# A two-layer graph network on one core: block order on TensorE, an earlier target term, and a cast that changes engine

## The reference

```
def _mp_layer(x, src, dst, edge_attr, W, b):
    # self loops with zero edge_attr are appended: src2, dst2, ea2
    msg = concat([x[dst2], x[src2], ea2], axis=1) @ W + b
    agg = segment_sum(msg, dst2, num_segments=n)
    return relu(agg)
h   = relu(_mp_layer(x, src, dst, edge_attr, W1, b1))     # 64 -> 128
out = _mp_layer(h, src, dst, edge_attr, W2, b2)           # 128 -> 64
y   = log_softmax(out, axis=1)
return layernorm(x + y, axis=-1)
```

## Time and profile before

| what | value |
|---|---|
| profiled execution, device time | 207.35 us |
| its span in the trace | 205.5 us |
| median of three runs | 207.33 us |
| PE busy, matmul | 174.7 us (85%) |
| DVE busy | 174.2 us (85%) |
| ACT busy | 118.8 us (58%) |
| POOL busy | 49.6 us (24%) |

### The profile page before, as it was taken

How to read it: one execution, slowest core, us unless ns; L and a number is a source line. 1 busy time by engine, 2 the same in 40 slices (tenths; PEclk the granted TensorE clock), 3 DMA queues, 4 the chain that set the end, 5 groups by cost and what they waited for, 6 DMA issues and landing times.

```text
span 205.5 us, 5089 instructions
## 1 busy us (share of the span) xinstructions
PE 174.7 (85%) x2019; PEld 162.7 (79%) x2019; DVE 174.2 (85%) x495; ACT 118.8 (58%) x234; POOL 49.6 (24%) x58
## 2 busy tenths in 40 slices
PE   0414489899999999999899999999996999999940
PEld 0103389778989999889789999898996999999940
DVE  1899999999999999999999989921029999999873
ACT  2236658679898998898798989984310201121101
POOL 8388998403200594006004000000000000000000
PEclk9999999999999999999999999999999999999995
DMA  1334101000000000000000000000000010011000
GB/s 42 102 85 131 25 0 40 0 4 2 3 0 4 0 5 0 3 1 3 0 4 0 5 0 3 2 3 0 3 0 0 3 35 6 6 38 25 22 22 20
DMA packets 8886, 3.32 MB, mean 16 GB/s; under 512 B 8146, under 2 KB 8411, under 8 KB 8861
## 3 DMA queue, kind: packets, MB, share of 16 engines
q1 hardware_dynamic: 8061, 2.04, 4.8%
q0 software_dynamic: 800, 0.93, 1.8%
HBM read 2.15 MB, written 0.81 MB: 14 GB/s over the span
## 4 chain that ended last, share of the span: by engine, by line
DVE 51%; PE 38%; issue 4%; ACT 2%; DMA 2%; ACTq 0%; DVEq 0%
PE pset L1022 17%; DVE ohr L517 17%; DVE ohl L517 16%; PE acc L1022 7%; PE acc L981 6%; PE pset L967 4%; DVE adj L507 3%; DVE u L548 2%; DMA adj<-in_dst 2%; DVE adj L466 1%; PE epb L1008 1%; PE epb L1016 1%; PE epb L996 1%; DVE x L533 1%; DVE u L556 1%
## 5 line engine op out<-in xcount | busy, mean ns | idle before, releaser
L820 ACT ACTIVATE adj<-pset 125x1000 bf16<-125x1000 f32 (+7 forms) x100 | 81.1, 836 | 14.1 <-PE pset L967 12.0
L981 PE MATMUL acc<-x,adj 125*125 125x195 bf16 x625 | 67.4, 250 | 0.0
L967 PE MATMUL pset<-ohr,ohl 128*125 128x125 bf16 x625 | 53.9, 230 | 9.2 <-DVE ohr L517 8.7
L967 PEld LDWEIGHTS pset<-ohr,ohl 128*125 128x125 bf16 x625 | 48.0, 145 | 14.9 <-issue 5.8
L981 PEld LDWEIGHTS acc<-x,adj 125*125 125x125 bf16 x625 | 56.7, 138 | 0.3
L517 DVE TENSOR_TENSOR ohl<-iota,keys 128x1000 bf16<-128x1000 bf16 (+1 forms) x79 | 52.4, 664 | 0.6 <-ACT keys L803 0.5
L517 DVE TENSOR_TENSOR ohr<-iota,keys 128x1000 bf16<-128x1000 bf16 (+1 forms) x79 | 52.5, 664 | 0.0
L1022 PE MATMUL pset<-z,adj 125*125 125x192 bf16 x425 | 36.9, 246 | 1.8 <-DVE x L665 1.8
L1022 PEld LDWEIGHTS pset<-z,adj 125*125 125x125 bf16 x425 | 35.6, 136 | 2.4 <-DVE x L665 2.0
L909 ACT ACTIVATE x<-x 125x192 f32<-125x192 f32 (+2 forms) x6 | 2.6, 428 | 34.5 <-DVE x L674 34.5
L387 POOL CAST stats<-se 125x15 bf16<-125x15 f32 x5 | 4.8, 952 | 52.8 <-DMA se<-se_scratch 52.8
(11 more groups left out here) (122 smaller groups left out, 171.4 us busy)
## 6 DMA issues: line engine op xcount, KB each, us to landing
x_nat<-in_x_tiles SPq DMA_DIRECT2D x1, 406.2 KB
x_nat<-in_x_tiles SPq DMA_DIRECT2D x1, 375.0 KB
out<-x SPq DMA_DIRECT2D x2, 187.5 KB
out<-x SPq DMA_DIRECT2D x3, 93.8 KB
adj<-in_dst SPq DMA_DIRECT2D x1, 208.5 KB
out<-x SPq DMA_DIRECT2D x1, 125.0 KB
adj<-in_edges,adj POOLq DMA_INDIRECT x5, 4.9
adj<-in_edge_attr,adj POOLq DMA_INDIRECT x5, 3.4
```

What stands on the lines that cost most here:

```text
L820: ins = act.activation(adj4[0:Q, g, :, i * WD:(i + n) * WD].rearrange("p h (w e) -> p h w e", e=WD), rows[:, w - k * SET:w - k * SET + n, ...
L967: ins = pe.matmul(pset[k % 2][0:Q, i // 4, i % 4 * 128:i % 4 * 128 + WD * G], ohl[k % 3][:, i // 2, :, i % 2], ohr[k % 3][:, i // 2, :, i ...
L981: ins = pe.matmul(acc[g % 2][0:Q, 0:XW], adj4[0:Q, g, h, :], x3[:, h, :], start=(h == 0), stop=(h == G - 1))
```

## The change

Five edits, in the order of the program:

- the cast of the targets is made by ScalarE (an activation with a bias) where it was a VectorE operation;
- on VectorE `onehots(4)` moves in front of `attr_sums(0)`, which moves behind `low_of_x(1)`;
- on TensorE `layer1` of block b stands in front of `build(b + 4)`, for every block, and the wait of group 0 on x is split in two;
- `base_of` is called for groups 0 to 11 and 12 to 15 right after the last `reduce_sums`, and for 16 to 24 after the first batch; the wait on `rest_ready` in front of it goes;
- the last step of a batch is one subtraction and one multiplication over all its groups, with the subtraction put between two small operations on the variance.

```diff
-            dve.tensor_scalar(rows16[:, 0:EC], dst_rows[:, 2:EC + 2], -float(MID), None, ALU.add).then_inc(rowsf_ready, 1)
...
-            attr_sums(0, 0, WD)
             onehots(3)
             low_of_x(1, XA, G)
-
-            for k in range(4, NSETS):
+            onehots(4)
+            attr_sums(0, 0, WD)
+
+            for k in range(5, NSETS):
...
             reduce_sums(G - 1)
+            dve.wait_ge(b2_in, 16 * 2)
+            for j in range(J):
+                dve.wait_ge(se_in[j], 16)
+            base_of(0, BATCHES[1][1])
+            base_of(BATCHES[1][1], BATCHES[2][1])
             z_rest(last - 1)
...
-            dve.wait_ge(rest_ready, len(EPILOGUES))
-            base_of(0, BATCHES[1][1])
...
-                flink(dve.tensor_tensor(r, y, y, ALU.mult))
+                fpost(dve.tensor_tensor(r, y, y, ALU.mult))
+                dve.wait_ge(fch, fc[0] - 1)
+                flink(dve.tensor_tensor(o, p, c.unsqueeze(2).broadcast_to([Q, n, C]), ALU.subtract))
...
-                for k in range(n):
-                    ins = dve.tensor_scalar(f_v[i % 2][:, k, :], f_p[:, k, 0:C], f_c[:, k:k + 1], f_r[:, k:k + 1],
-                                            ALU.subtract, ALU.mult)
-                flink(ins)
+                flink(dve.tensor_tensor(vv, o, r.unsqueeze(2).broadcast_to([Q, n, C]), ALU.mult))
...
-                    base_of(BATCHES[1][1], G)
+                    base_of(BATCHES[2][1], G)
...
+            act.wait_ge(dst_in, 16)
+            act.activation(rows16[:, 0:EC], dst_rows[:, 2:EC + 2], ACT.Copy, bias=-float(MID)).then_inc(rowsf_ready, 1)
...
                     if g == 0:
-                        pe.wait_ge(xl_ready, 2)
+                        pe.wait_ge(xm_ready, 1)
+                        pe.wait_ge(xl_ready, 1)
                         pe.wait_ge(keys_ready, 1)
...
+                    if g == 0 and h == XA:
+                        pe.wait_ge(xm_ready, 2)
+                        pe.wait_ge(xl_ready, 2)
...
             for b in range(NSETS):
-                if b + LEAD < NSETS:
-                    build(b + LEAD)
                 i, end = b * SET, b * SET + set_size(b)
                 while i < end:
...
+                if b + LEAD < NSETS:
+                    build(b + LEAD)
```

More of the change, by code:

```diff
@@ L619, in _ @@
             z_low(last - 2)
[L620 to L625, removed]
             fc = [0]
@@ L650, in base_of @@
                 flink(dve.tensor_tensor(base[:, a:b, :], base[:, a:b, :], late_part, ALU.add))
+            reduce_sums(G - 1)
             dve.wait_ge(b2_in, 16 * 2)
@@ L654, in _ @@
                 dve.wait_ge(se_in[j], 16)
-            dve.wait_ge(rest_ready, len(EPILOGUES))
             base_of(0, BATCHES[1][1])
+            base_of(BATCHES[1][1], BATCHES[2][1])
+            z_rest(last - 1)
+            z_low(last - 1)
+            z_rest(last)
+            z_low(last)
+            dve.tensor_reduce(deg_sum[:, :], stats[:, :, 0], AX.X, ALU.add).then_inc(deg_ready, 1)
             na = 0
```

## The result

| | kernel before | changed kernel |
|---|---|---|
| median device time | 207.29 us (207.03 to 207.69) | 223.21 us (222.76 to 223.76) |
| ratio to before, 95% interval | | 1.0768 (1.0753 to 1.0784) |
| profiled execution, its span | 207.35 us, 205.5 us | 223.76 us, 222.0 us |
| PE / DVE / ACT busy | 174.7 / 174.2 / 118.8 us | 177.8 / 175.9 / 119.0 us |

A forecast was written before the change was run, and what follows sets the result against it. VectorE (51%) and TensorE (38%) were taken to share the chain, TensorE with 7 us spare in the loop. Sum: 207.35 + 18.1 (waits) - 0.5 (start) - 1.07 (cast) - 1.81 (target) - 0.13 (last step) = 222.0 us; range 213 to 230.

The forecast's parts named there:

- What bounds the kernel: Layer-1 loop: VectorE and TensorE share the chain; TensorE has 7 us to spare, 5.0 of it for new waits.
- Group starts: Layer 1 of groups 1 to 24 waits for ScalarE's evacuation, no longer covered by other TensorE work: 19.2 us in sum.
- price 1.36 - 0.086 p: Wait in us of a group that begins p matmuls into its layer-1 block, until its evacuation is done.
- turn_sums: Epilogues in the loop: its wait of about 0.25 us for scale_x grows by 0.69 in six; +3.9 us.
- Head start: Start of the loop: layer 1's block 0 runs ahead of build 4, while TensorE waits for one-hots; -0.5 us.
- The order of attr_sums: Start, on VectorE: moving attr_sums(0) leaves the sum of work up to one-hot 5 as it was; nothing.
- The cast: Start: with dst cast on ScalarE, VectorE begins its picks at once and TensorE starts sooner; -1.07 us.
- Target term: Layer 2: base_of fits VectorE's hole of 5.91 us, and TensorE's wait ahead of group 6 goes; -1.81 us.
- Last step: End of the last batch: the stretch of 1.35 us becomes 1.22; -0.13 us.
- Hidden waits: Rival for the loop: VectorE bounds it, TensorE's new waits cost nothing, and the kernel takes 204.3 us; 7%.
- The clock: Rival for the loop: pauses at each group drop TensorE to 1.2 GHz for a third of 75 sets; +15, 237 us; 5%.
- backlog: Rival for the loop: ScalarE falls behind, 15 group starts each meeting one more cast; +7.5, 229.5 us; 12%.

The follow-up runs named there:

- build-first version: Changed kernel with one edit undone, build(b + 4) again in front of layer 1 of block b in all blocks: 204.63 us, ratio 0.9867.
- the kernel with block 0 alone: Changed kernel with layer 1 in front of the build in block 0 only and the build first in blocks 1 to 78: 204.78 us, ratio 0.9875.
- last experiment: Changed kernel with build(b + 4) again in front of layer 1 in all blocks and the cast of dst back on VectorE: 205.34 us, ratio 0.990.

## Why the prediction was right

By its own steps:

- *What bounds the kernel.* 7 us of spare time for TensorE was the number that decided, and the traces bear it out. From the first layer-1 matmul to the first of layer 2 the build-first version took 115.2 us and the changed kernel 135.1, that is 19.8 more. The new waits in this stretch are 25.0 us (20.4 + 5.3 - 0.7) less the 1.4 of group 0, which lie ahead of it: 23.6. The stretch also holds one build more, about 0.9 us, since layer 1 of block 0 now begins before it. So about 4.7 us were absorbed; 5.0 had been allowed. Between 27.1 and 141.3 us the kernel before has above all these waits of builds, and the changed kernel has none from its first layer-1 matmul on:

```profile
PE pset L967 <- DVE ohr L517: 2.3, 5, 0.8
PEld pset L967 <- ACT adj L820: 3.1, 7, 1.0
```

- *Group starts.* Forecast 19.2 us in 24 places, measured 20.4 in 22 by the idle time of the weight loads, of which one is group 0's own 1.4: 19.0 for the rest. (The rows of the matmuls give 16.2 in 20, since their modelled ends reach into the wait.) By the distances between starts the three parts of the forecast come out one by one: 16.2 us for the 16 groups that pay in full (16.3 forecast), 1.7 for the seven behind an epilogue (2.1), 0.7 for group 24 (0.8). The price 1.36 - 0.086 p holds where it was read: 1.25 us at p = 1 (1.27 by the list), and 78.30 + 0.17 to 79.64, 1.17, at p = 2 (1.19).

```profile
78.30 0.33 PE L986 MATMUL acc<-x,adj 125*125 125x195 bf16 x2
...
79.64 0.56 PE L986 MATMUL acc<-x,adj 125*125 125x195 bf16 x4 [1.01 <-ACT adj L821]
```

- *turn_sums.* Forecast +3.9 us in six epilogues, measured 0.7 to 5.3 in six, +4.6. The wait that it had before was read too large: 8 x 0.25 = 2.0, where the list has 0.7 in three.
- *Head start.* Forecast -0.5. Layer 1 does begin 0.8 us sooner than in the build-first version (24.79 against 25.61), but by the kernel with block 0 alone it is worth nothing in the end.
- *The order of attr_sums.* Forecast nothing, and nothing it is: 0.85 us won at the first layer-1 matmul, together with the split wait on x, and 1.14 lost behind it (last experiment). The prediction did not see that the loop would be the longer for it.
- *The cast.* Forecast -1.07, and the start gained 0.56. This term was mis-sized by half. The step that failed is that VectorE would be done with its picks by as much sooner as the cast had taken. The first pick took 0.64 us where the same shape takes 0.25 later. All 14 traces show why the length of the operation did not matter: what VectorE begins at that moment ends at a fixed time. The cast on VectorE began at 4.55 to 4.87 us in five traces, took 1.20 to 0.89, and ended at 5.75 to 5.77 in each. With the cast on ScalarE the first pick began at 4.66 to 5.04 in seven traces, took 0.92 to 0.54, and ended at 5.57 or 5.58 in each; in the other two it ended at 5.21, and the first row matmul came at 5.75 instead of 6.11, which is the 0.91 us of the cast alone. So it did not matter either that the targets landed 0.13 us later in this execution (4.73 against 4.60). GpSimd has a row of memsets from 4.25 to 5.5 us in all of them (to 5.6 in those two); that it is the cause was not tested.
- *Target term.* Forecast -1.81, measured -2.3 alone, and -2.13 for the whole last part with the last step's 0.13 in it.
- *Last step.* Forecast 1.22 us, measured 1.21. Alone it can't be told from nothing, as its size said. By the estimate from the rule of the Trainium skill ("VectorE: DVE Perf Modes", the perf-mode tier table) it would have lost 0.1 us; the trace has it 0.14 shorter than the 1.35 before.
- *The rivals.* Hidden waits (204.3 us) is what the kernel gives once the order is undone, 204.6, so its price was right and its condition was not met. The clock stayed at its upper level: the granted clock is 1.00 from 31 to 160 us, and a build takes 72.98 to 73.47, 0.49 us, right between pauses of a microsecond. With six sets ahead it did fall, so the rival's mechanism exists in this kernel, at pauses of 1.6 to 1.9 us. For the slow first blocks (0.86 us for a build) the prediction names the lower level; the profile gives 1.00 for 27.0 to 29.7 us, so that reading rests on the spacing alone. ScalarE had no backlog; over 64 to 84 us its busy time fell from 18.00 to 14.70.

The net: +18.63 at the first layer-2 matmul was forecast as +16.5 (-1.07 - 0.5 + 18.1). The loop grew by 21.0 us (114.1 to 135.1) and not by 18.1, and its start came 2.35 us sooner and not 1.57. The 2.9 us in the loop are about 0.5 of waits, 0.3 less absorbed, 0.9 for the build that moved into it, and 1.1 that the order of `attr_sums` gives back. So the result within 0.6% of the forecast owes something to luck: two errors of opposite sign, 2.9 and 0.8 us.

## What to carry to other kernels

In a software pipeline over serial engine lists, moving a consumer by one place against its producers changes the cover of every wait in the loop, not that of the first round alone: list what stands between each producer and its consumer, and price the difference against the spare time of the engine that waits. Where two engines are both near full, spare time is a few per cent and a wait of one evacuation in each group costs nearly all of itself. A lead can be too long as well as too short: another engine's list may have its consumers at fixed places. And an operation that is only put off makes the next stage begin sooner without making it end sooner; compare a later event, too.

## What the runs showed of the hardware or the kernel that I had not expected

- A lead of five sets costs 2.1% and one of six 17.8%, with VectorE waiting 12.1 and 42.6 us for layer 1's end.
- At the start a VectorE operation ended at a fixed time whatever it was and whenever it began: a cast of 0.89 to 1.20 us at 5.76 in five traces, a pick of 0.54 to 0.92 us (0.25 later) at 5.58 in seven of nine.
- TensorE's granted clock fell to 0.50 for 3.4 us twice in the kernel with six sets ahead, after pauses of up to 1.9 us; it stayed at 1.00 in the changed kernel's loop, whose matmul rows show pauses of up to 1.2 us.
- An edit that gained nothing alone in the timed runs (the cast, 0.9995) was probably worth about 0.3% beside the others; in both pairs of traces the whole of its head start lasts through the loop.
